# Factorization-machine kernel: the 84-row remainder of the input as one transfer or as eight, before or behind the first group

## The reference

```python
x_reg = input_data @ W_lin.T + b_lin
emb = input_data @ factors                      # 12500 -> 16
sum_squared = jnp.square(emb.sum(axis=1))
squared_sum = (jnp.square(input_data) @ jnp.square(factors)).sum(axis=1)
h = jax.nn.relu(emb @ W1.T + b1)
h = jax.nn.relu(h @ W2.T + b2)
dnn_out = h @ W3.T + b3
x = x_reg + 0.5 * (sum_squared - squared_sum)[:, None] + dnn_out
x = 0.5 + jax.nn.sigmoid(x) * 5.0
```

## Time and profile before

| | before |
|---|---|
| median of three runs | 136.48 us |
| the profiled execution, its own time | 136.62 us |
| span of that execution's trace | 134.3 us |
| PE busy | 106.3 us (79%) |
| ACT busy | 65.1 us (48%) |
| DVE busy | 53.4 us (40%) |
| data queue (q1), share of 16 DMA engines over the span | 92.8% |
| mean rate over the span | 389 GB/s |

### The profile page before, as it was taken

The page is one execution under the profiler, slowest core; times in us unless marked ns, Lnnn a source line. Parts: engine busy times, 40 slices in busy tenths (PEclk is TensorE's granted clock), DMA queues, the critical chain, the costliest instruction groups (busy, mean ns, idle before and its releaser), DMA issues.

```text
span 134.3 us, 2688 instructions
## 1 busy us (share of the span) xinstructions
PE 106.3 (79%) x1034; PEld 29.9 (22%) x1034; DVE 53.4 (40%) x52; ACT 65.1 (48%) x74; POOL 11.6 (9%) x49
## 2 busy tenths in 40 slices
PE   6089976965976966967978969977977889889991
PEld 1022211111211111111112312211211123336760
DVE  0391550450550451352351393152253155555840
ACT  4030752661752652562573496372473374447741
POOL 5026011011011011011011001111000000000000
PEclk9999999999999999999999999999999999999999
DMA  4999999999999999999999999999999999999500
GB/s 120 394 366 439 420 439 415 434 410 439 420 439 420 439 420 439 420 434 424 429 429 420 439 420 434 420 429 424 429 429 429 418 412 427 428 403 411 193 5 1
DMA packets 4580, 52.25 MB, mean 389 GB/s; under 512 B 518, under 2 KB 650, under 8 KB 1502
## 3 DMA queue, kind: packets, MB, share of 16 engines
q1 hardware_dynamic: 4574, 52.16, 92.8%
HBM read 52.16 MB, written 0.00 MB: 388 GB/s over the span
## 4 chain that ended last, share of the span: by engine, by line
DMA 62%; PE 29%; SPq 2%; issue 2%; DVE 2%; ACT 1%; DVEq 0%; ACTq 0%
DMA xr<-in_x_groups 53%; PE p_lin L427 22%; DMA xr<-in_x_end 10%; PE p_tot L427 2%; PE p_sq L427 2%; PE p_h L508 2%; DVE sq L362 1%; SPq L212 1%; PE p_h L532 1%; ACT sg L302 1%; SPq L210 0%; SPq L209 0%; SPq L208 0%; ACT lin L288 0%; ACT qs L338 0%
## 5 line engine op out<-in xcount | busy, mean ns | idle before, releaser
L275 ACT ACTIVATE sq<-xr 128x1536 f32<-128x1536 f32 (+1 forms) x40 | 48.5, 1263 | 47.5 <-DMA xr<-in_x_groups 47.4
L362 DVE TENSOR_TENSOR sq<-xr 128x1536 f32<-128x1536 f32 x20 | 35.1, 1758 | 56.9 <-DMA xr<-in_x_groups 56.9
L427 PE MATMUL p_lin<-xr,wr 128*17 128x512 f32 x320 | 38.3, 594 | 16.2 <-DMA xr<-in_x_groups 16.2
L427 PE MATMUL p_lin<-sq,wz 128*18 128x512 f32 x320 | 38.4, 595 | 2.7 <-DVE sq L362 1.2
L427 PEld LDWEIGHTS p_lin<-xr,wr 128*17 128x17 f32 x320 | 8.1, 97 | 45.3 <-POOL wr L250 24.7
L427 PEld LDWEIGHTS p_lin<-sq,wz 128*18 128x18 f32 x320 | 8.3, 97 | 32.3 <-ACT sq L275 19.5
L283 ACT ACTIVATE sq<-xr 128x384 f32<-128x384 f32 (+1 forms) x17 | 9.6, 617 | 6.7 <-DMA xr<-in_x_end 6.7
L250 POOL COPY wr<-hd x20 | 5.9, 296 | 73.8 <-PE p_lin L427 73.3
L369 DVE TENSOR_TENSOR sq<-xr 128x640 f32<-128x640 f32 (+1 forms) x15 | 9.8, 695 | 6.2 <-DMA xr<-in_x_end 6.2
L427 PE MATMUL p_lin<-xr,hd 128*17 128x320 f32 (+1 forms) x128 | 8.9, 381 | 0.9 <-DMA xr<-in_x_end 0.9
L427 PE MATMUL p_lin<-xf,hd 128*17 128x512 f32 x4 | 3.6, 1049 | 3.7 <-DMA xf<-in_x_first 3.7
(11 more groups left out here) (49 smaller groups left out, 36.6 us busy)
## 6 DMA issues: line engine op xcount, KB each, us to landing
xr<-in_x_groups SPq DMA_DIRECT2D x20, 2048.0 KB, 15.4
xr<-in_x_end SPq DMA_DIRECT2D x4, 1280.0 KB, 13.4
xr<-in_x_end SPq DMA_DIRECT2D x3, 768.0 KB, 13.6
hd<-in_head SPq DMA_DIRECT2D x1, 934.0 KB, 4.7
xr<-in_x_end SPq DMA_DIRECT2D x1, 576.0 KB, 14.5
xf<-in_x_first SPq DMA_DIRECT2D x1, 512.0 KB, 5.9
xl<-in_x_rest SPq DMA_DIRECT2D x1, 336.0 KB
xr<-in_x_end SPq DMA_DIRECT2D x1, 192.0 KB, 14.5
```

Of the source, the lines that this page charges most:

```text
L275: nc.scalar.activation(sq[:, s, c:c + n, :], xr[:, s, c:c + n, :], ACT.Square).then_inc(act_squared, 1)
L362: nc.vector.tensor_tensor(sq[:, s, 0:BY_DVE, :], xr[:, s, 0:BY_DVE, :], xr[:, s, 0:BY_DVE, :], ALU.mult).then_inc(dve_squared, 1)
L427: return nc.tensor.matmul(out, lhsT, rhs, start=False, stop=False, skip_group_check=True)
```

## The change

The remainder's one transfer becomes eight, of 14, 13, 12, 11, 10, 9, 8 and 7 rows (84 in all, from the last rows to the first), and they are issued behind the first group and ahead of the second. VectorE and TensorE wait for all eight. The bytes are the same, and no instruction of another engine moves.

```diff
+REST_CUT = tuple(range(14, 6, -1))
+assert sum(REST_CUT) == REST
...
             sp.dma_start(xf[:, :], x_first).then_inc(first_landed, 16)
-            sp.dma_start(xl[0:REST, :], x_rest).then_inc(rest_landed, 16)
             for s in range(RING):
                 sp.dma_start(xr[:, s].rearrange("p c b -> p (c b)"), x_groups[s, :, 0:CHUNKS * HALF]).then_inc(x_landed[s], 16)
+                if s == 0:
+                    for n in REST_CUT:
+                        rows = slice(n * (n - 1) // 2 - REST_CUT[-1] * (REST_CUT[-1] - 1) // 2,
+                                     n * (n + 1) // 2 - REST_CUT[-1] * (REST_CUT[-1] - 1) // 2)
+                        sp.dma_start(xl[rows, :], x_rest[rows, :]).then_inc(rest_landed, 16)
...
-            dve.wait_ge(rest_landed, 16)
+            dve.wait_ge(rest_landed, 16 * len(REST_CUT))
...
-            pe.wait_ge(rest_landed, 16)
+            pe.wait_ge(rest_landed, 16 * len(REST_CUT))
```

## The result

| | before | changed |
|---|---|---|
| median of 20 runs each | 136.63 us | 137.12 us |
| lowest, highest | 136.36, 136.92 | 136.71, 137.67 |
| profiled execution, its own time | 136.62 | 137.11 |
| span | 134.3 | 134.9 |

The ratio is 1.0032, with a 95% interval of 1.0024 to 1.0040: 0.44 us slower (the medians lie 0.49 apart). In a second comparison, on another occasion, it was 1.0027 (1.0015 to 1.0038). The scatter has grown from 0.56 to 0.96 us. The forecast was 136.05 us, 0.43 faster.

What follows compares the result with a forecast made beforehand. DMA landings were taken to bound the kernel; -0.46 (row counts) + 0.03 (completions) + 0 + 0 gave -0.43 us, from 136.48 to 136.05 us. Its own range was 135.7 to 136.2, that of all cases 135.5 to 137.2.

Steps and rivals of the forecast that it cites:

- What bounds the kernel: Whole kernel: DMA landings set the end; all landings earlier by d move the end by d.
- Speed of the remainder's rows: While the remainder is fetched: 336 GB/s against 428, 0.32 us lost for all engines, taken as unchanged: 0.
- The rival of crowding: Remainder's rows to neighbouring partitions: engines 0 to 6 4.0 us behind, 1.5 us in hand, up to 139.0 us; chance 0.16.
- Eight transfers, the row counts: Remainder's rows per engine: fewer on engines 9 to 13, up to two more on 0 to 7; end moves -0.46 us.
- X: Late DMA engine, read as one of fourteen hit by the 82 us instruction packet, 1.5 us behind peers; three rows less.
- The forecast step to group 12: ScalarE's step at 82.66 to 88.28: its 0.72 us extra should shrink by about 0.4.
- Completions: Engines 0 to 6 end eight transfers where they ended one: 0.03 us taken.
- Later landing of the remainder: Remainder lands near 13.8 us instead of 8.7; TensorE catches up before 40 us, DMA queue does not run dry: 0.
- SyncE: Seven more issues of about 0.46 us put groups 1 to 3 back by 3.2 us; hidden.
- The sum: Whole kernel: -0.46 + 0.03 + 0 + 0 = -0.43 us.

Runs made afterwards that it cites:

- e5: Against the kernel before: remainder as six transfers of 14 neighbouring rows behind the first group, six rows on each of engines 0 to 13; 137.38 us, ratio 1.0057.
- e6: Against the kernel before: remainder as six transfers of 14 rows, six partitions apart, behind the first group; 136.62 us, ratio 0.9999.
- e7: Against the kernel before: remainder padded with 44 zero rows to 128, one transfer at its old place; 136.28 us, ratio 0.9970.
- e12: Repeat against the kernel before: eight transfers of 14 down to 7 rows, nine partitions apart over 128, behind the first group; 136.04 us, ratio 0.9965.
- e11: Against the kernel before: six transfers of 14 rows, nine partitions apart over 128, behind the first group; 136.19 us, ratio 0.9967.
- e9: Against the kernel before: eight transfers of 14 down to 7 rows, nine partitions apart over 128, behind the first group; 135.82 us, ratio 0.9932.
- e1: Against the kernel before: remainder still one transfer of 84 rows, but moved behind the first group; 136.66 us, ratio 1.0003.
- e2: Against the kernel before: remainder as six transfers of 14 rows, six partitions apart, ahead of the first group; 137.68 us, ratio 1.0075.
- e13: The changed kernel once more, against the kernel before; 136.97 us, ratio 1.0027.
- e3: Against the kernel before: remainder as six transfers of 14 neighbouring rows ahead of the first group; 137.36 us, ratio 1.0070.
- e8: Against the kernel before: remainder as two transfers, of 80 rows and 4 rows, at the old place; 136.66 us, ratio 1.0003.

## Why the prediction was wrong

**What bounds the kernel** held. The DMA engines set the end, and the lateness of group 3 and the pieces is the lateness of the end.

**Speed of the remainder's rows** is the first step that failed. I took the slow stretch "as it is, the nearest row: 0". It grew from 0.53 to 0.98 us in the profile, 0.45 more (0.33 more by single packets), and e5 against e6 shows what drives it: whether one transfer's rows go to neighbouring partitions, worth 0.76 us of the time there. The stretch of 336 GB/s was in my rows, and I priced it as a constant although the change alters exactly what stands in it. The single transfer had a weaker form of the same thing: e7, whose transfer covers the same 128 partitions as a group's, gained 0.3% in spite of two rows more on fourteen engines and eight on the other two.

**The rival of crowding** was the right mechanism, at the wrong place and size. It put 4.0 us on engines 0 to 6 and let 1.5 us of slack absorb most. In fact the delay falls on all engines at once, so there is no slack to absorb it: the two earliest engines are late too. (Its threshold was also miscounted: 1.5 us of slack is used up from 0.15 us more per row on, not 0.19, since two of the eight rows are new.) The Trainium skill, "SBUF — State Buffer", section on the DMA port swizzle, would let a transfer to 14 neighbours reach four or five ports. The direction agrees with 245 GB/s for neighbours and 382 for rows six apart (e5, e6); no run here shows a port by itself. The source side is not what tells e5 from e6, since both read neighbouring rows; whether it adds to the slow stretch was not tried.

**Eight transfers, the row counts**, is the second step that failed: -0.46 forecast, from X gaining three rows. No gain that can be told from zero was measured side by side. X lies 0.65 us behind the earliest engine before and after; on one occasion e12 and e11, which differ in the counts, are at 0.9965 and 0.9967; and the last engine is farther behind the middle in every profile with falling counts than in those with six rows on 14 engines. That the changed kernel (1.0032, 1.0027) lies below e5 (1.0057) does not speak for the counts, since e5's stretch is also slower (245 GB/s against 288 and 266, which is 0.30 and 0.15 us of the 0.34 and 0.41 between them), and e5's interval reaches down to 1.0035. Only e9's occasion (0.9932) leaves room for the forecast gain. The forecast step to group 12, shorter by 0.4 us, was shorter by 0.2 in the one profile and level in the other (5.62 before; 5.42, 5.67). Whether uneven counts widen the scatter is not shown either: 0.96 us in the changed kernel's 20 runs, but 0.90 in e5's six with even counts and 0.34 in e12's five with uneven ones.

**Completions**, 0.03: nothing seen (e6 level with e1), but 0.03 is below what the runs tell apart. **Later landing of the remainder**, 0: held; e1 is 1.0003, and TensorE caught up at 33 us, though group 4 was issued at 22.82 us, later than the worst case of 22.2. `sql` started at 14.03 for the 13.8 forecast, group 0 at 12.69 for 12.6. **SyncE**, hidden: held behind group 0, and e2 shows what it costs without that cover.

**The sum**: +0.45 from the slow stretch (0.61 by e13's) and about nothing from the counts give +0.45; measured +0.44. A gain of 0.4 from the counts with 0.8 from crowding would give the same time, but neither profile of the changed kernel shows 0.8 lost.

## What to carry to other kernels

When a transfer's shape is changed, look at the rate in the stretch where the old one ran: if it is already below the steady rate, the new shape may change that, and here it slowed every engine's transfers, not only its own. Cutting the transfer into small ones cost nothing for the completions here, but lay the rows of each apart, and put them where their issue is covered; or, simpler, pad the transfer to all partitions (e7). Where a straggler decides the end, find it in the trace before giving it less work: completion packets show each engine's place.

## What the runs showed of the hardware that I had not expected

- Rows of 4 KB to neighbouring partitions held the whole core's DMA rate at 245 GB/s over 3 us (e5), with all engines busy; the same rows six apart ran at 382 (e6). The group packets that started meanwhile took up to 1.5 us in e5 and up to 0.95 in e6, against 0.61 in the steady stretch.
- Issuing a transfer of 14 rows took SyncE 0.83 us with partitions six or nine apart (e2, e6, e11) and 0.48 to 0.50 us with neighbours (e3, e5).
- An instruction packet costs the engine that carries it 1.56 us (kernel before, packets at 29 and 82 us): 1.02 to 1.09 us of its own, and the group packet that starts as it ends takes 1.09 to 1.16 instead of 0.61. Where all engines are level (e7, e8) the first such packet delays a group by 1.4 us and the next, on another engine, delays none.
